# A new table of likings and of step costs for the planner that orders four engines and the DMA queue

## The reference

```python
x = x + attn_a(layernorm(x))   # 16 heads of 16, causal over 1024 keys, W1/b1/Wp/bp
x = x + ffn(layernorm(x))      # silu(x@wg.T) * (x@wu.T) @ wd.T, hidden 768, int weights / 127
x = x + attn_b(layernorm(x))   # 16 heads of 16, a sliding window of 64 keys, 63 of them given at the start
x = x + ffn(layernorm(x))      # the same weights again
```

## Time and profile before

| | us |
|---|---|
| median of 3 runs (1525.37 to 1531.69) | 1528.34 |
| the profiled execution's own time | 1531.69 |
| its span | 1530.0 |
| PE busy | 1298.8 (85%) |
| DVE busy | 935.2 (61%) |
| ACT busy | 787.9 (51%) |
| POOL busy | 388.3 (25%) |

### The profile page before, as it was taken

One profiled execution on the slowest core, in us unless ns is written; L12 is line 12 of the kernel. 1 busy time (PEld: TensorE's weight loads), 2 busy tenths in 40 slices (PEclk: granted clock), 3 DMA queues, 4 the chain that ended last, 5 costly groups with the idle time before them and its releaser, 6 DMA issues.

```text
span 1530.0 us, 24911 instructions
## 1 busy us (share of the span) xinstructions
PE 1298.8 (85%) x9601; PEld 814.6 (53%) x9601; DVE 935.2 (61%) x1628; ACT 787.9 (51%) x1122; POOL 388.3 (25%) x383
## 2 busy tenths in 40 slices
PE   2688988897888988899788898889798898889967
PEld 2543337764763335765674333776476333477656
DVE  4369745574658783566556974456565888246733
ACT  2254674455544566446355467345544456634542
POOL 1321123311442123211234112231134212331122
PEclk9989999998999999999899999899899999889989
DMA  7530121423260012253324012133425101215130
GB/s 291 175 104 16 50 71 49 125 79 121 90 185 20 15 58 77 84 133 91 122 83 128 16 50 71 49 99 99 121 96 167 38 9 64 64 58 154 50 112 28
DMA packets 103525, 134.40 MB, mean 88 GB/s; under 512 B 29057, under 2 KB 88769, under 8 KB 100161
## 3 DMA queue, kind: packets, MB, share of 16 engines
q1 hardware_dynamic: 103392, 132.57, 28.5%
HBM read 51.45 MB, written 11.61 MB: 41 GB/s over the span
## 4 chain that ended last, share of the span: by engine, by line
PE 60%; ACT 12%; DVE 10%; DMA 7%; issue 5%; POOL 3%; SPq 3%; POOLq 0%; ACTq 0%; DVEq 0%
PE opsum L1198 10%; PE ring L1168 9%; PE ring L1147 8%; ACT probs L996 6%; PE ring L1234 6%; DVE peak L758 6%; PE ring L1235 6%; PE ring L1124 5%; PE opsum L1254 3%; PE opsum L1259 3%; DMA on_lo<-onf 3%; PE ring L1057 2%; ACT L938 1%; PE ring L1093 1%; DVE xt_lo L732 1%
## 5 line engine op out<-in xcount | busy, mean ns | idle before, releaser
L758 DVE TENSOR_REDUCE peak<-ring 128x1 f32<-128x640 f32 (+5 forms) x480 | 472.7, 1006 | 151.5 <-PE ring L1124 147.9
L996 ACT ACTIVATE probs<-ring 128x1024 f32<-128x1024 f32 (+3 forms) x480 | 399.2, 852 | 262.3 <-PE ring L1168 108.0
L1147 PE MATMUL ring<-k_st,q_st 96*128 96x192 bf16 (+4 forms) x1280 | 246.7, 298 | 34.1 <-ACT probs L996 11.8
L1168 PE MATMUL ring<-q_st,k_st 98*128 98x512 bf16 (+5 forms) x1408 | 249.3, 290 | 18.0 <-DMA q_st<-peak_b 6.6
L1198 PE MATMUL opsum<-probs,V 128*32 128x512 f32 (+5 forms) x2816 | 232.3, 412 | 15.6 <-POOL probs L689 14.8
L1234 PE MATMUL ring<-xt_hi,w_gu_sb 128*128 128x512 f32 x384 | 165.2, 430 | 39.5 <-DVE xt_lo L732 26.6
L695 POOL TENSOR_TENSOR onf<-onf,o_hi 128x512 fp32r<-128x512 f32 x64 | 81.4, 1273 | 428.9 <-ACT o_hi L1015 428.9
L1168 PEld LDWEIGHTS ring<-q_st,k_st 98*128 98x128 bf16 (+1 forms) x1408 | 97.2, 99 | 165.4 <-ACT probs L996 57.3
L700 POOL TENSOR_TENSOR h_lo<-hid,h_hi 128x512 fp32r<-128x512 f32 x96 | 122.2, 1286 | 222.1 <-ACT h_hi L1033 221.7
L1147 PEld LDWEIGHTS ring<-k_st,q_st 96*128 96x128 bf16 x1280 | 100.4, 98 | 145.1 <-ACT probs L996 58.3
L1235 PE MATMUL ring<-xt_lo,w_gu_sb 128*128 128x512 f32 x384 | 162.6, 423 | 1.5 <-issue 1.5
(11 more groups left out here) (113 smaller groups left out, 1842.0 us busy)
## 6 DMA issues: line engine op xcount, KB each, us to landing
q_st<-q_part SPq DMA_DIRECT2D x192, 128.0 KB, 2.4
w_gu_sb<-img_gu SPq DMA_DIRECT2D x16, 1536.0 KB, 7.8
k_st<-k_part SPq DMA_DIRECT2D x144, 128.0 KB, 2.4
w_qkv<-img_qkv SPq DMA_DIRECT2D x8, 1536.0 KB, 6.4
on_hi<-o_hi SPq DMA_DIRECT2D x64, 128.0 KB, 2.7
on_lo<-onf SPq DMA_DIRECT2D x64, 128.0 KB, 2.8
k_st<-k_part SPq DMA_DIRECT2D x48, 144.0 KB, 2.5
x_next<-in_x SPq DMA_DIRECT2D x4, 1024.0 KB, 5.9
```

The lines of the kernel that those rows point to most:

```text
L758: dve.tensor_reduce(dst, heads_of(slot_of(a, e), unit, plan.a_width(i)), AX.X, ALU.max).then_inc(a_max, 1)
L996: act.activation(probs[0:rows, n % 2, h:h + heads, 0:w], heads_of(slot_of(a, e), unit, w)[0:rows], ACT.Exp).then_inc(exp_done, 1)
L1147: pe.matmul(flat(slot)[:, per * n + c:per * n + c + d], q, k_st[p][0:SP_ROWS, head, first_key + c:first_key + c + d], start=(per * n % 512 ...
L1168: last = pe.matmul(flat(slot)[0:rows, per * n:per * n + w], k_st[p][:, head, first_key:first_key + rows], q_st[p][:, hf, head, q0 - HALF * ...
```

## The change

It changes numbers only: both tables of likings, and the costs in `Plan.steps`. No instruction's work changes; what changes is the order on each engine and the ring slots. After it the lines below L60 stand 2 further down.

```diff
 LIKES = (
-    dict(T=1, N=1, V=0.2, O=3.44, L=0.19, w=3.55, W=0.3, Z=-0.09, H=0.08, M=0.03, J=-0.83, I=-0.62, lead=1.25,
-         ahead=1.22, late=-0.25, A=0.66, B=0.43, G=-0.4, Q=2.34, P=0.74, S=-0.34, K=-1.71, R=0.3, C=0.21, Y=1.48),
+    dict(T=1.0, N=1.0, V=0.53, O=0.11, L=0.02, w=2.0, W=0.3, Z=0.15, H=0.26, M=0.77, J=0.05, I=0.2,
+         lead=1.25, ahead=1.04, late=-0.25, A=0.66, B=0.17, G=0.0, Q=2.34, P=0.74, S=-0.83, K=0.5,
+         R=0.3, C=-0.31, Y=1.2),
...
             w = heads * self.b_width(e[1] // 4, j)
-            return ([("PE", 0.00043 * w * (1 if self.causal else 2), 0.2), ("ACT", 0.26 + 0.00073 * w, 0.07)]
-                    + [("POOL", 0.64, 0.05)] * self.masked_on_pool(e[1], e[2]))
+            return ([("PE", 0.03 + 0.00043 * w * (1 if self.causal else 2), 0.1), ("ACT", 0.2 + 0.00071 * w, 0.1)]
+                    + [("POOL", 0.64, 0.1)] * self.masked_on_pool(e[1], e[2]))
...
         if kind in "wW":
-            return [("PE", 2.9, 0.2), ("DVE", 1.7 if self.causal == (kind == "W") else 0.7, 0.1)]
+            return [("PE", 4.4, 0.1), ("DVE", 2.1 if self.causal == (kind == "W") else 0.7, 0.1)]
...
-                "Z": [("ACT", 0.21, 0.05), ("DVE", 1.6, 0.1)],
+                "Z": [("ACT", 1.5, 0.2), ("DVE", 1.8, 0.1)],
```

More of the change, by code:

```diff
@@ L55 @@
 LIKES = (
-    dict(T=1, N=1, V=0.2, O=3.44, L=0.19, w=3.55, W=0.3, Z=-0.09, H=0.08, M=0.03, J=-0.83, I=-0.62, lead=1.25,
-         ahead=1.22, late=-0.25, A=0.66, B=0.43, G=-0.4, Q=2.34, P=0.74, S=-0.34, K=-1.71, R=0.3, C=0.21, Y=1.48),
-    dict(T=2.7, N=0.01, V=0.2, O=0.06, L=0.52, w=3.86, W=-0.66, Z=0.33, H=0.04, M=0.18, J=0.2, I=0.06, lead=2.23,
-         ahead=0.45, late=-1.05, A=0.44, B=0.17, G=0.55, Q=2.25, P=1.26, S=-0.36, K=-1.81, R=0.3, C=0.03, Y=1.9))
+    dict(T=1.0, N=1.0, V=0.53, O=0.11, L=0.02, w=2.0, W=0.3, Z=0.15, H=0.26, M=0.77, J=0.05, I=0.2,
+         lead=1.25, ahead=1.04, late=-0.25, A=0.66, B=0.17, G=0.0, Q=2.34, P=0.74, S=-0.83, K=0.5,
+         R=0.3, C=-0.31, Y=1.2),
+    dict(T=2.07, N=-0.17, V=0.51, O=0.25, L=0.07, w=1.73, W=-1.01, Z=0.31, H=0.5, M=0.3, J=0.2,
+         I=0.11, lead=1.95, ahead=0.22, late=-0.82, A=0.8, B=-0.03, G=0.0, Q=2.25, P=1.63, S=-1.02,
+         K=-0.67, R=0.3, C=-0.17, Y=2.07))
 def running(counts):
@@ L170, in steps @@
             w = heads * self.a_width(i)
-            mask = 0.055 if self.causal else 0.082
-            return [("PE", mask * heads + 0.00043 * w, 0.2), ("DVE", 0.16 + 0.00104 * w, 0.05)]
+            mask = 0.06 if self.causal else 0.085
+            return [("PE", 0.03 + mask * heads + 0.00043 * w, 0.1), ("DVE", 0.09 + 0.00104 * w, 0.1)]
         if kind == "B":
@@ L175, in steps @@
             w = heads * self.b_width(e[1] // 4, j)
-            return ([("PE", 0.00043 * w * (1 if self.causal else 2), 0.2), ("ACT", 0.26 + 0.00073 * w, 0.07)]
-                    + [("POOL", 0.64, 0.05)] * self.masked_on_pool(e[1], e[2]))
+            return ([("PE", 0.03 + 0.00043 * w * (1 if self.causal else 2), 0.1), ("ACT", 0.2 + 0.00071 * w, 0.1)]
+                    + [("POOL", 0.64, 0.1)] * self.masked_on_pool(e[1], e[2]))
         if kind == "V":
-            return [("PE", 0.02 + 0.0016 * self.b_width(e[1] // 4, e[2]), 0.2)]
+            return [("PE", 0.1 + 0.00105 * self.b_width(e[1] // 4, e[2]), 0.15)]
         if kind in "wW":
-            return [("PE", 2.9, 0.2), ("DVE", 1.7 if self.causal == (kind == "W") else 0.7, 0.1)]
+            return [("PE", 4.4, 0.1), ("DVE", 2.1 if self.causal == (kind == "W") else 0.7, 0.1)]
         if kind == "S":
@@ L184, in steps @@
         if kind == "P":
-            return [("PE", 2.9 if e[1] < 2 else 0.75, 0.2), ("ACT", 1.1 if e[1] < 2 else 0.4, 0.1)]
+            return [("PE", 3.0 if e[1] < 2 else 0.8, 0.1), ("ACT", 1.0 if e[1] < 2 else 0.4, 0.1)]
         if kind == "F":
             return [("SP", 0.6, {"wp": 3.0, "gu": 6.0, "qkv": 6.0, "store": 4.0, "x": 4.0}[e[1]])]
-        return {"Q": [("PE", 2.75, 0.2), ("ACT", 1.3, 0.05), ("DVE", 1.4, 0.1)],
[2 rows of a table removed]
+        return {"Q": [("PE", 2.75, 0.1), ("ACT", 1.3, 0.1), ("DVE", 1.45, 0.1)],
[2 rows of a table added]
                 "C": [("ACT", 0.6, 0.1), ("SP", 0.6, 2.2)], "R": [("DVE", 0.25, 0.1), ("SP", 0.6, 2.2)],
[2 rows of a table removed]
-                "Z": [("ACT", 0.21, 0.05), ("DVE", 1.6, 0.1)],
-                "L": [("PE", 0.9, 0.2), ("ACT", 1.02, 0.05), ("DVE", 1.22, 0.15)],
-                "G": [("PE", 1.82, 0.2), ("ACT", 0.6, 0.05)], "I": [("DVE", 0.7, 0.1)],
-                "J": [("ACT", 0.62, 0.1), ("POOL", 1.29, 0.1)], "x": [("POOL", 5.5, 0.1)],
[2 rows of a table added]
+                "Z": [("ACT", 1.5, 0.2), ("DVE", 1.8, 0.1)],
+                "L": [("PE", 0.9, 0.1), ("ACT", 1.05, 0.1), ("DVE", 1.25, 0.1)],
+                "G": [("PE", 1.65, 0.1), ("ACT", 0.6, 0.1)], "I": [("DVE", 0.7, 0.1)],
+                "J": [("ACT", 0.63, 0.1), ("POOL", 1.3, 0.1)], "x": [("POOL", 5.5, 0.1)],
                 "k": [("POOL", 0.5, 0.1)]}[kind]
```

## The result

| | before | after |
|---|---|---|
| median (us) | 1528.88 (1525.37 to 1531.69, 4 runs) | 1571.67 (1567.78 to 1575.43, 4 runs) |
| ratio, 95% interval | | 1.0281 (1.0245 to 1.0317) |
| span of the profiled execution | 1530.0 | 1571.4 |

A forecast was written before the change was run, and what follows sets the result against it. PE, busy 85%, was taken as the bound, so a new order counts only where PE stands or runs slow. Seams 9.0, sliding layers 0.8 and causal layers 1.6 gave +11.4 us: 1540 against 1528.34, range 1519 to 1568.

The forecast's parts named there:

- What bounds, and that it gets slower: Whole kernel: PE busy 85%, so order matters only in its waits and lower-clock stretches; slower given 0.62.
- Seam: Sliding to causal layer, layers 2, 4, 6: Q0.0 starts 3.5 us later for L5's slot; 3.0 each, 9.0 in all.
- The upper bound: At the seam: 4.9 us, from 3.5 and some 1.4 for products at 1.2 GHz after the wait.
- The lower bound: At the seam: about zero, since V0.0 waits for POOL; on that path alone it moves 1.3 us or less.
- Start of a sliding layer: Four times: new wait of 4.0 at A0.0 replaces 2.54 at w1.0; +1.7 us at B0.0, bounds 0 and +4.0.
- V nearer to B: Groups 0 to 5 of a sliding layer: nine V wait 0.39 each, +3.5 us a layer, bounds zero and 4.
- End of a sliding layer: B6.0 to G0 takes 22.1 us instead of 26.1; with 1.0 for the clock, -5.0 a layer, bounds -8 and -2.
- Middle of a causal layer: From walking groups 1 and 4: +0.8 us for groups 0 to 3 and -0.3 for 4 to 7.
- the rival: V waits add up in causal layers: 40 us on top of 11, 1579; chance 0.12.
- End of a causal layer: End of its attention: Z2's two table loads cost V7.6 and V7.7 the full 3.0; +0.7 us net a layer.
- Gate and up: Causal layer: packing lands in time for O1, which waited 2.38, but W0.0 waits for POOL; -0.8 us a layer kept.
- The range: 1519 to 1568 us, taking in most of the sliding end's case and upper bounds of seam and causal layers together.

The follow-up runs named there:

- new_causal_only: Causal layers planned with the new likings and costs, sliding layers with the old ones; ratio 1.0030 to the kernel before, 4.6 us above it.
- other_seam_slot: Changed kernel with ring slots turned so that Q0.0 of causal layers takes G11's slot, not L5's; ratio 1.0178 to the kernel before.
- old_sliding_start: Changed kernel, but sliding layers begin with the old lists of all engines up to B0.1 on PE; ratio 1.0133 to the kernel before.
- new_sliding_end: Kernel before, with the changed kernel's lists and slots from B6.0 on in sliding layers and slots turned at the seams; ratio 0.9974.

## Why the prediction was wrong

- *What bounds, and that it gets slower:* right. PE's waits (28.6 us) and the lower clock (12.8) are all there is in the 41.4 us.
- *Seam:* the wait was right (3.5 us later, 4.02 in all, at L5's low part, in layers 2, 4, 6). The term is the one that was mis-sized: 3.0 each forecast, 5.3 on average up to B0.0. The upper bound named 1.4 for slow products; they are the rule here (1.6 at each seam), not the bound. The 1.07 at w1.0, which was to go against it, does so only under the old causal order (+1.0 us in sum). In the new one Q1.0 stands ahead of w1.0, which waits for nothing even where the seam has no wait (new_causal_only), so there was nothing to set off. The lower bound took V0.0 to wait for POOL, but the row has no wait; other_seam_slot won 15.8 us, so no such path hid the seam.
- *Start of a sliding layer, the step that failed:* "At B0.0 I get 1.0 later with one A (0.67) still to do: +1.7". Measured +4.8 to +6.0 with that A still to do. The walk had the wait of 4.0 right; what stood behind it was taken to wait for nothing more and to run at the full clock. For layer 3 the traces give it as 2.8 us more waiting (7.6 against 4.8), 2.9 more in slow products (4.2 against 1.3 at w1.0) and 0.7 of an A less: 5.0, against 4.8 measured. In the waiting, the 0.76 and 1.59 us at T0 and Q0.1 were not seen: L1's low part stands behind four maxima, Z1 and four more on DVE. This term alone misses by 18 of the 30 us between the sum and the traces, and old_sliding_start gives 22.6 us back. Its upper bound was +4.0, too low, since neither those waits nor a price of the lower clock was in it. The rest of the 30, by the table: groups 0 to 5 of causal layers 11, the seam 7, the stretch behind G0 5, the end of sliding layers 3; the other rows came out 14 lower than forecast.
- *V nearer to B:* the mechanism right (each of the nine V waits, for ACT), 2.1 instead of 3.5; each waits 0.24 and not 0.39. With the one A more that these groups take over from the start, the forecast is 16.7 in all, against 11.7 measured.
- *End of a sliding layer:* B6.0 to G0 in 21.7 to 22.0 us, forecast 22.1; V7.6 waits 2.03, forecast 2.3. The extra 1.0 for the clock was not there.
- *Middle of a causal layer:* +0.5 forecast, +3.3 a layer measured. Groups 1 and 4 were walked and 2 and 3 not, which are 2.0 longer in layers 2, 4 and 6. It wasn't the rival either, which gave some 40 us: causal layers alone cost 4.6. Which pair of lists makes the 2.0 us is open.
- *End of a causal layer:* +0.7 forecast, -0.9 measured on average. The Trainium skill (ScalarE: Activation LUTs, What ACT_TABLE_LOAD costs) would have made that term about 3, an estimate from its drain at each switch. The traces don't agree: a load takes 1.28 us and its first use 0.20, both loads of Z2 3.0 in the earlier trace rows, and no drain is seen.
- *Gate and up:* the wait at O1 went, as forecast, and came back at W0.0 (G5 to W0.0 is 7.3 us in layer 2 before and after). Forecast -0.8 a layer; measured +2.3 to -2.8 in the four causal layers, -0.3 on average, with slow products coming and going.
- *The range* was built from bounds of single waits. Both large terms, the seam and the start, have a second price in slow products, and they were added as if there were none.

## What to carry to other kernels

Where PE is the bound and a change of order adds a wait of some microseconds on it, price the wait with the slow products behind it, from a place of the same trace where such a wait stands (here w1.0: 2.54 us of waiting, and in two of four layers 1.3 us more in the products); where the price comes only sometimes, it belongs at least in the upper bound. Ask of every shorter stage which queue sets the next wait: here a table load in front of two copies took back what a better order of DMAs had won, and one move on ACT gave 10 us. Splicing two orders at points where both have done the same set of steps is a cheap way to find out which stretch carries a difference. The parts needn't add up: here the two halves of the change cost 29 us and the whole 43.

## What was not expected of the hardware

A wait of 4.2 to 5.0 us cost 2.0 to 2.6 us more behind it (A0.0 to A1.0: 7.8 to 8.3 us in the changed kernel, 5.7 without slow products). Filling it with 14 products whose results nobody reads took this away where 1.15 and 1.6 us of the wait stayed and not where 1.9 and 2.0 stayed, and where it did, it also removed the slow stretch 13 us later, behind a wait of 1.6 us that was still there. The same wait at the same place isn't always followed by slow products: behind 2.42 us at W0.0 four of eight events of the changed kernel took 4.5 to 4.6 us, and the others 3.1. What decides it is open. The same kernel's runs differ with the mean granted clock: of ten runs of new_sliding_end the fastest took 1521.75 us at a mean clock of 0.966 and the slowest 1538.47 at 0.951. With such a spread, a difference under 0.5% can't be told here from a few runs.
